# Key weights and context loaded and multiplied ahead of the fourth token tile in a two-layer attention and expert kernel

## What is computed

```python
x = x + relu_attention(layernorm(x), ctx)      # q, k, v projections with relu; relu scores
x = x + fp6_ffn(layernorm(x))                  # both operands quantised in blocks of 32
x = x + (layernorm(x) @ W1.T + mean(ctx) @ W2.T + b)
x = x + expert_choice_ffn(layernorm(x))        # 16 experts, top 128 tokens each, three layers

def relu_attention(q, c):
    qp = relu(q @ Wq + bq)
    kp = relu(c @ Wk + bk)
    vp = relu(c @ Wv + bv)
    s = relu(qp @ kp.T) / sqrt(512) + mask
    return relu(s @ vp)
```

## Time and profile before

| | us |
|---|---|
| median of 3 runs | 766.11 (765.79 to 766.21) |
| the profiled execution | 765.68 |
| its span in the profile | 763.9 |
| outside the span | 1.78 |
| PE busy in the span | 698.9 (91%) |
| DVE busy | 566.5 (74%) |
| POOL busy | 431.0 (56%) |
| ACT busy | 388.8 (51%) |

### The profile page before, as it was taken

How to read it: one execution, slowest core, us unless ns; L and a number is a source line. 1 busy time by engine, 2 the same in 40 slices (tenths; PEclk the granted TensorE clock), 3 DMA queues, 4 the chain that set the end, 5 groups by cost and what they waited for, 6 DMA issues and landing times.

```text
span 763.9 us, 12387 instructions
## 1 busy us (share of the span) xinstructions
PE 698.9 (91%) x4380; PEld 618.2 (81%) x4380; DVE 566.5 (74%) x1004; ACT 388.8 (51%) x591; POOL 431.0 (56%) x599
## 2 busy tenths in 40 slices
PE   6999999999999999999995029999999999999993
PEld 5766888888888888888884028999999999999992
DVE  5786789888898988877987983666666666666651
ACT  5755355445444444445553204566666666665550
POOL 2635788888888888777782703244433333333331
PEclk9999999999999999999997558999999999999997
DMA  9600122221222122111115705388888878777743
GB/s 307 250 29 14 42 83 82 74 70 57 97 81 85 60 85 70 42 57 46 68 57 190 236 2 164 126 238 240 235 234 243 236 238 244 225 226 223 207 79 45
DMA packets 53902, 102.89 MB, mean 135 GB/s; under 512 B 5392, under 2 KB 6480, under 8 KB 53840
## 3 DMA queue, kind: packets, MB, share of 16 engines
q1 hardware_dynamic: 46672, 85.31, 33.9%
q0 software_dynamic: 7168, 16.78, 9.9%
HBM read 76.68 MB, written 25.17 MB: 133 GB/s over the span
## 4 chain that ended last, share of the span: by engine, by line
PE 45%; DMA 19%; issue 18%; DVE 10%; POOL 4%; ACT 2%; POOLq 0%; DVEq 0%; ACTq 0%
PE bank L260 24%; DMA out<-y,ids 18%; PE bank L267 5%; PE banks L609 4%; PE banks L615 3%; PE banks L260 2%; PE banks L619 2%; PE banks L620 2%; DVE pack L1620 1%; DVE left L1630 1%; DVE pos L1622 1%; DVE bn L1280 1%; POOL xd L1917 1%; POOL x L1923 0%; PE banks L507 0%
## 5 line engine op out<-in xcount | busy, mean ns | idle before, releaser
L1978 POOL DMA_INDIRECT out<-y,ids x32 | 76.2, 2380 | 171.4 <-DVE y L1788 166.5
L1292 DVE TENSOR_TENSOR w_l<-w_raw,w_h 128x2048 fp32r<-128x2048 f32 x45 | 103.0, 2289 | 31.3 <-ACT w_h L985 31.3
L1243 ACT ACTIVATE h<-bank,b 128x512 f32<-128x512 f32 x64 | 44.0, 687 | 107.4 <-PE bank L260 107.4
L1292 DVE TENSOR_TENSOR hT_l<-h,hT_h 128x512 fp32r<-128x512 f32 x64 | 44.2, 691 | 66.9 <-ACT hT_h L1249 66.9
L985 ACT ACTIVATE w_h<-w_raw 128x2048 fp32r<-128x2048 f32 x48 | 90.6, 1924 | 2.1 <-DMA w_raw<-w 2.1
L1280 DVE BATCH_NORM_STATS2 bn<-x 128x6 f32<-128x512 f32 x119 | 81.9, 688 | 8.2 <-DMA x<-x 5.2
L260 PE MATMUL bank<-tokT_l,w_h 128*128 128x256 f32 x256 | 72.4, 283 | 0.0
L260 PE MATMUL bank<-hT_h,w_h 128*128 128x256 f32 x256 | 72.4, 283 | 0.0
L260 PE MATMUL bank<-tokT_h,w_h 128*128 128x256 f32 x256 | 72.4, 283 | 0.0
L260 PE MATMUL bank<-tokT_h,w_l 128*128 128x256 f32 x256 | 72.4, 283 | 0.0
L260 PE MATMUL bank<-hT_l,w_h 128*128 128x256 f32 x256 | 72.4, 283 | 0.0
(11 more groups left out here) (291 smaller groups left out, 2177.5 us busy)
## 6 DMA issues: line engine op xcount, KB each, us to landing
w_raw<-w SPq DMA_DIRECT2D x48, 1024.0 KB, 6.3
x<-x SPq DMA_DIRECT2D x32, 256.0 KB, 2.8
out<-x SPq DMA_DIRECT2D x32, 256.0 KB, 2.0
xn<-xn SPq DMA_DIRECT2D x32, 256.0 KB, 2.0
mask<-mask_t SPq DMA_DIRECT2D x8, 256.0 KB, 3.2
stage<-wk SPq DMA_DIRECT2D x1, 1024.0 KB, 8.3
stage<-wq SPq DMA_DIRECT2D x2, 512.0 KB, 8.2
stage<-wf SPq DMA_DIRECT2D x1, 1024.0 KB, 10.4
```

Of the source, the lines that this page charges most:

```text
L1243: act.activation(h32[n % 2][:, :], ps_hid[n % 4][:, :], ACT.Relu, bias=bias)
L1292: dve.tensor_tensor(dst, src, hi_part, ALU.subtract).then_inc(sem, 1)
L1978: pool.indirect_dma_start(out=out_rows, out_offset=bass.IndirectOffsetOnAxis(ap=ids[:, r:r + 1], axis=0), in_=y[e % 2][b][:, :], in_offset ...
```

## The change

SP loads the context and the key weights directly behind tile 2, and tile 3 and the gate weights behind them. PE gets 13 dummy matmuls ahead of everything else, and the dummies now read `mean_w` (there since the first us) instead of `ident` (a load). The first chunk of the keys moves ahead of the transposes of tile 3, the other three directly behind them, and the gate means go last, behind all keys. `T` is renumbered to that order. DVE takes the low part of tile 0 ahead of the sums of tile 3. DVE's `setup("wgc")` stays where it was.

```diff
-    T = counts("wgm k0 k1 k2 k3 v0 wf0 wf1 wf2 wf3 v1 ...")
+    T = counts("k0 k1 k2 k3 wgm v0 wf0 wf1 wf2 wf3 v1 ...")
...
         load_x(1)
-        sp.dma_start(wgf[:, :, 0:E], chunked(io.wg)).then_inc(sm.c_wg, 16)
         load_x(2)
-        load_x(3)
         sp.dma_start(ctx_raw[:, :, :], chunked(io.ctx_t)).then_inc(sm.c_ctx, 16)
         sp.dma_start(stage[1][:, :, :], chunked(io.wk)).then_inc(sm.c_wk, 16)
+        load_x(3)
+        sp.dma_start(wgf[:, :, 0:E], chunked(io.wg)).then_inc(sm.c_wg, 16)
...
-                pe.matmul(ps_q[0][:, 0:P], ident[:, :], ident[:, :], start=True, stop=True)
+                pe.matmul(ps_q[0][:, 0:P], mean_w[:, :], mean_w[:, :], start=True, stop=True)
+
+        pe.wait_ge(sm.g_set, GS["mean"])
+        warm_up(13)
         t1(0)
         warm_up(3)
         t1(1)
         warm_up(3)
         t1(2)
+        keys((0,))
+        t1(3)
+        keys((1, 2, 3))
         gate_means()
-        t1(3)
-        keys()
         q_chunk(*q_of(0))
...
         stats1(2)
+        lo1(0)
         stats1(3)
-        lo1(0)
         lo1(1)
```

More of the change, by code:

```diff
@@ L363, in build @@
     V = counts("wgc wq0 wq1 wf8 va0 v0 wf0 wf1 wf2 wf3 va1 mean wc0 wc1 v1 w1g wc2 wc3 cbcol cg")
-    T = counts("wgm k0 k1 k2 k3 v0 wf0 wf1 wf2 wf3 v1 wc0 wc1 gt w1g wc2 wc3 crow col row0 cg row1")
+    T = counts("k0 k1 k2 k3 wgm v0 wf0 wf1 wf2 wf3 v1 wc0 wc1 gt w1g wc2 wc3 crow col row0 cg row1")
     GS = counts("half mean k01 k23 wf")
@@ L661, in logit_rows, with keys @@
                 last.then_inc(sm.p_seg, 1)
-        def keys():
+        def keys(chunks):
             pe.wait_ge(sm.c_ctx, 16)
             pe.wait_ge(sm.c_wk, 16)
-            for c in range(C):
+            for c in chunks:
                 e = slice(c * P, (c + 1) * P)
```

## The result

| | before | changed |
|---|---|---|
| median | 765.95 us (4 runs, 765.70 to 766.21) | 772.38 us (4 runs, 772.16 to 773.02) |
| ratio | | 1.0087, 95% interval 1.0075 to 1.0099 |
| profiled execution | 765.68, span 763.9 | 773.02, span 771.2 |

The change costs 6.4 us, 0.9%.

What follows compares the result with a forecast made beforehand. Bound by the prologue chain from DVE's `wq_l`, with no PE slack later; dummies 0, tile 2's gain 0, DVE held behind the keys +6.9, rounded to +7: 766.11 + 7.0 = 773.1 us, range 770.4 to 775.8.

Steps and rivals of the forecast that it cites:

- The load order: Prologue loads: tile 3 lands at 12.2 us, the key weights about 0.6 earlier at 11.6.
- The hold: DVE's gate correction waits for gate means behind all keys, so `wq_l` starts at 22.25 instead of 15.31: +6.9 us.
- Rival A: Tile 3 lands by about 9.5, its transposes directly behind the first key chunk: +4.8 at `wq_l`, 770.9 us; chance 0.13.
- Rival B: PE loses its full rate in the gaps ahead of tile 3 or the queries: 775 to 778 us; chance 0.09.
- both gaps are shorter than 3 us: PE's waits of 2.1 us ahead of tile 3 and 2.7 ahead of the queries, so a rate fall is less likely.
- Rival C: PE's order decides, not DVE's hold: a gain of up to 2 us, 764.1 us; chance 0.02.
- Rival D: The shift meets slack later in the first phase: same as before to 770 us; chance 0.04.
- the stretch from there to the end as before: From the end of the first phase, itself 7 us later, to the kernel's end: time unchanged.
- The 0.7 us: Prologue: dummies move tile 2's transposes from 11.33 to about 10.6, a gain that ends in the wait for tile 3.

Runs made afterwards that it cites:

- e2: The changed kernel with DVE's gate correction moved behind the query weights, the sums of tiles 4 and 5 and the FFN scales: 767.33 us, ratio 1.0029.
- e3: The changed kernel with the gate means ahead of tile 3's transposes, in PE's gap behind the first key chunk: 767.61 us, ratio 1.0033.
- e4: The changed kernel without the 13 dummy matmuls at the start: 772.43 us, ratio 1.0088 to the kernel before.
- e6: The kernel before with only the 13 dummies at the start and all dummies on the constant `mean_w`: 765.05 us, ratio 0.9994.
- e5: The changed kernel with the loads in the old order, tile 3 and gate weights ahead of context and key weights: 772.39 us, ratio 1.0092.

## Why the prediction was right

It forecast 773.1 with a range of 770.4 to 775.8; 772.38 was measured, +6.4 for the forecast +7.0. The mechanism and its size are both as forecast. Step by step, in the changed kernel's profiled execution:

| step | forecast | trace |
|---|---|---|
| first transposes not delayed by the dummies | 6.75 | 6.73 |
| tile 2's transposes | 10.6 | 10.68 |
| key weights landed, first chunk starts | 11.6 | 11.54 |
| tile 3 landed | 12.2 | 12.0 (issue 3.61, 8.4 to landing) |
| tile 3's transposes | 15.4 | 15.23 |
| DVE's gate correction | 22.05 | 21.90 |
| DVE's `wq_l` | 22.25, +6.9 | 22.04, +6.73 |
| first query chunk | 24.6 | 24.50 |
| `t1(4)` | 29.0 | 28.77 |
| `t1(6)` | 37.3, +6.9 | 36.98, +6.61 |
| end of the first phase | +7 | +6.84 (the last transposes of the phase, 410.76 to 417.60) |

**The load order.** The rule used (tile 3 lands when the key weights landed before, since the same set of transfers stands ahead of it) was right within 0.2 us in this trace; in e2 and e3, with the same loads, tile 3 landed at 11.46 and 11.35, so part of that closeness is luck. DMA groups of the changed kernel: engine, op, count, KB, us to landing:

```profile
x<-x SPq DMA_DIRECT2D x1, 256.0 KB, 8.4
wg_pair<-wg SPq DMA_DIRECT2D x1, 32.0 KB, 8.1
```

The prediction also reads each landing in the kernel before as later than that of the load issued before it. That holds for the loads in its sum but not for all. The key bias, issued at 4.63 right behind the key weights, landed at about 11.9, ahead of their 12.4:

```profile
bk<-bk SPq DMA_DIRECT2D x1, 2.0 KB, 7.2
```

So here the order of issue alone did not fix the order of landing. Tile 3 did not overtake the key weights in any trace with the new order of loads.

**The hold.** The step that carries the sum was right, and the experiments show it from both sides: its single edit gives +6.8, half of it +2.4, and taking it out leaves +1.9 to +2.2. From tile 3 on each step is 0.1 to 0.3 us ahead of the forecast, as tile 3 was. That, the rounding from 6.9 to 7 and a median of 765.95 instead of 766.11 for the kernel before are of the size of the 0.7 us between 773.1 and 772.38; all are within what one trace or one set of runs leaves open.

**Rival A** (tile 3 early) didn't happen. Its price was near: the kernel with the old loads has +5.45 at `wq_l`, where A said +4.8; it had PE wait for tile 3 at 13.3 and not for the key weights, which land later when tile 3 is ahead of them (chunk from 12.20).

**Rival B** (PE loses its full rate in the gaps) didn't happen in the profiled execution: the 24 key records behind the first gap start 0.22 us apart (15.72 to 20.90), and the granted clock reads 1.00 from 22 to 28. But its second half, a fall ahead of the queries, did happen in e4, behind the same idle time of 2.63 us. The argument "both gaps are shorter than 3 us" therefore doesn't hold; what holds is the price, which was nothing at `t1(4)`. It may well be common: three of the four executions of the changed kernel have a mean granted clock of 0.958 to 0.959, as e4's profiled one with the fall has (0.959), while this one has 0.962 and none of the 56 recorded with the variants for the kernel before is under 0.960. All three are faster than this one, so if it fell there, it can't have cost much. **Rival C** (faster) asked for the hold to be off the path; kernels e2 and e3 show that even then the reordered loads leave it slower than before. **Rival D** (given back later) didn't happen either: +6.59 at 56 us, +6.84 at 410. PE's idle time between 85 and 130 us is 0.17 us, where the kernel before has none.

**What I had wrong** is "the stretch from there to the end as before", in what would show it. It isn't steady: it grew by 0.57 in the profiled execution, where the clock rises later ahead of the experts (+6.67 at the first dummy, +7.24 at the first expert matmul). That is nearly as large as the gap between forecast and result.

The 0.7 us that the prediction gives the dummies at tile 2 was in the changed kernel's trace (11.33 to 10.68), but e4 has 10.78 there without them. It doesn't touch the sum, which has them at 0.

## What to carry to other kernels

When an instruction's signal is moved later on one engine, find the instruction on the other engines that waits for it and read what is queued behind it there: here a 0.2 us correction that nobody waits for until the values' matmuls, some 19 us later in either kernel, held the one operation on the path, and moving it behind that operation takes away some 4.5 of the 6.4 us lost. The load that was pushed back landed about when the last of those now ahead of it used to land (12.0 and 12.4 us); ask which engine's queue stands behind it. And before trusting a gain at the start of a long kernel, check that both inputs of the next step come earlier, not just the engine: the 1.4 us by which tile 3's transposes were early in e6 became waits for two loads. And take one more trace of an unchanged prologue before crediting a few tenths to an edit.

## What the runs showed of the hardware

PE started its dummies at 1.01 us in each of the kernels that have them, and their records start 0.21 us apart at the lower rate, 0.11 at the full one. In e5 the spacing changed 3.5 us behind the first, in the changed kernel 4.8 us, and in e2 and e3 it didn't change within the burst at all: the last of the 26 records starts at 6.50, at the lower rate still. So the moment at which the full rate comes varied by at least 2 us behind the same unbroken work from the same start. Ahead of the experts, it came 3.3 to 6.1 us behind the first dummy.

The same idle time of PE, 2.63 us ahead of the first query chunk, left the full rate alone in the changed kernel and was followed by a fall from 24.2 to 27.6 in e4. Of 15 dummies in the gap at 446 us nothing was left at 455. A gain of half a us in the prologue of this kernel can't be told from such differences by the time of a few runs, and one trace tells it only if the loads landed as they did in the trace that it is compared with.
